# A graph network kernel: first edge tiles gathered at each group's first edge for the dense build

## The reference, cut to what matters

```python
dst = jnp.minimum((6250 * jax.random.uniform(key3, (200000,)) ** 2.0).astype(jnp.int32), 49999)
_o = jnp.argsort(dst, stable=True); src = src[_o]; dst = dst[_o]
...
x = _layernorm(x + _L0(x, src, dst, ...))     # three propagations: sum over edges of (x * norm)[src] into dst
x = _layernorm(x + _L1(x, edge_attr_64, ...)) # an MLP per edge, summed into dst
x = _layernorm(x + _L2(x, src, dst, w, ...))  # twice: segment_sum(w[:, None] * h[src], dst), then hyperbolic normalisation
x = _layernorm(x + _L3(x, src, dst, ...))     # one propagation with degree norms
```

## Time and profile before

| | us |
|---|---|
| median of 3 runs | 6,764.94 |
| lowest, highest | 6,760.87, 6,765.24 |
| the profiled execution | 6,769.59 |
| its span, first to last instruction | 6,767.8 |
| mean granted TensorE clock, share of full | 0.837 |

### The profile page before, as it was taken

One profiled execution on the slowest core, in us unless ns is written; L12 is line 12 of the kernel. 1 busy time (PEld: TensorE's weight loads), 2 busy tenths in 40 slices (PEclk: granted clock), 3 DMA queues, 4 the chain that ended last, 5 costly groups with the idle time before them and its releaser, 6 DMA issues.

```text
span 6767.8 us, 158522 instructions
## 1 busy us (share of the span) xinstructions
PE 4832.8 (71%) x47510; PEld 3804.9 (56%) x47511; DVE 3362.4 (50%) x6082; ACT 1317.2 (19%) x3392; POOL 2135.5 (32%) x3522
## 2 busy tenths in 40 slices
PE   0999988877777777998936666666666667657475
PEld 0777776666666667998924444444444433323275
DVE  7989888777777774012134444444444420020323
ACT  0122233445555552000011111111111100000100
POOL 1222222222222221000027777777777720000000
PEclk9999999999999998999965556555555579989887
DMA  1011123333343343988753333333333359969575
GB/s 36 19 52 56 57 68 100 105 116 123 123 140 122 125 137 127 388 345 337 283 108 79 79 78 78 78 78 79 79 79 79 79 190 418 379 276 418 233 289 194
DMA packets 443092, 1053.75 MB, mean 156 GB/s; under 512 B 129847, under 2 KB 286849, under 8 KB 414081
## 3 DMA queue, kind: packets, MB, share of 16 engines
q1 hardware_dynamic: 392770, 1000.83, 41.3%
q0 software_dynamic: 50176, 51.48, 4.1%
HBM read 809.69 MB, written 242.41 MB: 155 GB/s over the span
## 4 chain that ended last, share of the span: by engine, by line
PE 33%; POOL 19%; DVE 14%; issue 12%; DMA 11%; POOLq 7%; ACT 2%; SPq 1%; ACTq 1%; DVEq 0%; PEldq 0%; PEld 0%
POOL WORK L624 18%; PE banks L1525 13%; PE banks L1486 12%; DMA T<-dense_w 8%; POOLq L350 4%; PE banks L1517 3%; DVE T L828 3%; DVE T L835 2%; PE banks L1556 2%; DMA WORK<-table,idx 2%; POOLq L581 1%; ACTq L346 1%; POOLq L590 1%; POOL T L581 1%; DVE WORK L922 0%
## 5 line engine op out<-in xcount | busy, mean ns | idle before, releaser
L624 POOL DMA_INDIRECT WORK<-table,idx x1568 | 1486.6, 948 | 1357.1 <-DVE idx L928 879.6
L1525 PE MATMUL banks<-T 128*128 128x125 bf16 (+1 forms) x21696 | 1672.9, 226 | 48.0 <-DVE T L835 8.8
L1525 PEld LDWEIGHTS banks<-T 128*128 128x128 bf16 x21696 | 1447.2, 115 | 341.5 <-DVE T L835 326.1
L828 DVE TENSOR_TENSOR T<-T 128x750 bf16<-128x750 bf16 x1808 | 995.3, 550 | 457.8 <-PE banks L1525 319.2
L581 POOL TENSOR_TENSOR T<-T 128x12 f32 x1816 | 567.4, 312 | 1818.6 <-DVE T L835 1250.6
L835 DVE TENSOR_TENSOR T<-T 128x750 bf16<-128x750 bf16 x1808 | 1002.0, 554 | 62.0
L1517 PE MATMUL banks<-T 128*128 128x250 bf16 x3616 | 711.8, 278 | 411.6 <-DVE T L828 142.9
L1486 PE MATMUL banks<-WORK,T 125*128 125x192 bf16 (+1 forms) x10000 | 835.0, 247 | 61.2 <-DVE WORK L972 61.2
L1486 PEld LDWEIGHTS banks<-WORK,T 125*128 125x128 bf16 (+1 forms) x10000 | 832.4, 99 | 63.7 <-issue 59.2
L1443 PE MATMUL banks<-T,WORK 128*128 x1568 | 275.4, 294 | 768.3 <-DVE WORK L884 768.3
L1283 ACT ACTIVATE WORK<-banks 125x252 f32<-125x252 f32 x1250 | 477.4, 382 | 1541.3 <-PE banks L1525 1470.0
(11 more groups left out here) (339 smaller groups left out, 3474.4 us busy)
## 6 DMA issues: line engine op xcount, KB each, us to landing
T<-dense_c SPq DMA_DIRECT2D x200, 1562.5 KB, 8.3
T<-dense_w SPq DMA_DIRECT2D x200, 782.0 KB, 10.3
T<-dense_w SPq DMA_DIRECT2D x200, 780.5 KB, 10.4
dense_w<-WORK SPq DMA_DIRECT2D x250, 546.9 KB
WORK<-rel_rows SPq DMA_DIRECT2D x197, 256.0 KB, 3.7
WORK<-in_eaT SPq DMA_DIRECT2D x392, 128.0 KB, 3.5
dense_c<-T SPq DMA_DIRECT2D x13, 3125.0 KB, 10.5
dense_c<-ACC SPq DMA_DIRECT2D x12, 3125.0 KB, 10.7
```

The lines of the kernel that those rows point to most:

```text
L624: nc.gpsimd.indirect_dma_start(out=g_sb[:, u, c * D:(c + 1) * D], out_offset=None, in_=table, in_offset=bass.IndirectOffsetOnAxis(ap=idx[: ...
L828: V.tensor_tensor(planes[:, v, 0:HOTS].rearrange("p (k n t) -> p k n t", k=3, t=QUAD), iota2[:, 0:LO, :].unsqueeze(1).to_broadcast([P, 3, ...
L1525: last = T.matmul(banks[:, u, to - low // QUAD:to + LO + high // QUAD], keys[:, t, j, :], planes[:, v, first - low:past + high].rearrange( ...
```

## The change

Each group gets one tile that is gathered from HBM, its first tile. Groups of 128 edges or fewer get the 128 edges from the group's first edge on, so one tile holds them all. Larger groups get their first whole column, and their further columns as before come from SBUF. For this the range stage turns keys, lows and weights to rows (three numbers an edge, `RECORD`), ScalarE copies them, and SP stores them in HBM (`edges_dram`). Each set now has 125 rows of ten groups, by `q` = group modulo ten. For each set GpSimd fetches the columns in which groups begin and end (`ends`), VectorE finds the first and last edge in them (`ends_of`), and ten indirect DMAs gather the first tiles (`got_rows`); TensorE turns them back, ScalarE and VectorE put them in `firsts`, with keys relative to the group and the weight in three parts.

The dense build then runs in units of four groups (`UNIT`): VectorE makes the planes of four first tiles with one call each for one-hots and products; TensorE puts each in a PSUM bank of its own (eight banks, two units). Groups go in blocks of two. A block has as many further steps as its larger group needs; a step (`more`) takes one column of each of the two groups, prepared by two GpSimd subtractions. A group that needs fewer is pointed at empty columns. The loops over steps are dynamic on GpSimd, VectorE and TensorE, which read a table of offsets. ScalarE copies two banks at once and a store holds ten groups, in place of five. `xT` is loaded after the dense build, and `sel` filled there.

```diff
+sp.wait_ge(edges_copied, TURNED)
+sp.dma_start(edges_dram[0:full * P, :].rearrange("(t p) x -> p t x", p=P), edge_rows[:, 0:full, :, :].rearrange("p t e k -> p t (e k)")).then_inc(edges_stored, 16)
...
+sp.dma_start(X[:], xT).then_inc(x_loaded, 16)
...
+pool.wait_ge(edges_stored, 32)
+for q in range(SETS):
+    if q >= 2:
+        pool.wait_ge(range_step, at_range(0, f"members{q - 2}"))
+    pool.wait_ge(range_step, at_range(0, f"hi_int{q}"))
+    for h, col in enumerate((lo_int, hi_int)):
+        nc.gpsimd.indirect_dma_start(
+            out=ends[:, q % 2, h, :, :].rearrange("p e k -> p (e k)"), out_offset=None, in_=edges_dram,
+            in_offset=bass.IndirectOffsetOnAxis(ap=col[:, q:q + 1], axis=0)).then_inc(ends_landed[q % 2], 16)
+pool.wait_ge(range_step, at_range(0, "start_int"))
+for q in range(SETS):
+    nc.gpsimd.indirect_dma_start(
+        out=got_rows[:, q, :, :].rearrange("p e k -> p (e k)"), out_offset=None, in_=edges_dram.rearrange("c (e k) -> (c e) k", k=RECORD),
+        in_offset=bass.IndirectOffsetOnAxis(ap=start_int[:, q:q + 1], axis=0)).then_inc(firsts_landed[q], 16)
 nc.gpsimd.memset(ACC_full[3 * P // 4:P, :], 0.0).then_inc(tails_cleared, 1)
+nc.gpsimd.memset(T1_full[3 * P // 4:P, TURNED * (P // 2):NP], 0.0).then_inc(tails_cleared, 1)
...
+def take(s, b, deltas):
+    slot = pool.snap(s & (QRING - 1), min_val=0, max_val=QRING - 1)
+    at = []
+    for t in range(QUAD):
+        pool.reg_alu(col[t], s + deltas[QUAD * b + t], COLS, ALU.min)
+        at.append(nc.s_assert_within(pool.snap(col[t]), 0, COLS, skip_runtime_bounds_check_because="a column is never before the first"))
+    pool.wait_ge(more_products, s + 1)
     pool.sem_inc(quads_begun, 1)
-    nc.gpsimd.tensor_tensor(quads[:, ds(slot, 1), :, :].rearrange("p s k t -> p (s k) t"), lists[:, :, ds(col, QUAD)],
-                            starts[:, u, :].unsqueeze(2).to_broadcast([P, 6, QUAD]), ALU.subtract).then_inc(quad_taken, 1)
-
-with pool.Fori(0, GROUPS // SPAN) as i:
-    bounds = bounds_of(pool, i * SPAN, SPAN)
...
+    for b in range(BATCH):
+        with pool.If(offs[b + 1] > offs[b]):
+            with pool.Fori(offs[b], offs[b + 1]) as s:
+                take(s, b, row[BATCH + 1:])
+    pool.wait_ge(quad_taken, offs[BATCH] + 1)
...
+        fin(V.tensor_scalar(g_back[:, col], g_lo[:, col], 1.0, -1.0, ALU.max, ALU.mult))
+        at(f"back{q}")
+        fin(V.tensor_scalar(g_lo[:, col], g_back[:, col], float(COLS), None, ALU.add))
+        fin(V.tensor_scalar(lo_int[:, col], g_back[:, col], float(COLS), None, ALU.add))
+        at(f"from{q}")
+        fin(V.scalar_tensor_tensor(g_hi[:, col], g_lo[:, col], 1.0, g_hi[:, col], ALU.add, ALU.max))
+        at(f"up{q}")
+        fin(V.tensor_scalar(hi_int[:, col], g_hi[:, col], -1.0, None, ALU.add))
+
+    def ends_of(q):
+        col = slice(q, q + 1)
+        keys = ends[:, q % 2, :, :, 0]
+        dve.wait_ge(ends_landed[q % 2], 32 * (q // 2 + 1))
+        fin(V.tensor_scalar(met.rearrange("p (h e) -> p h e", h=2), keys, g_first[:, col], None, ALU.is_ge))
+        at(f"past{q}")
+        fin(V.scalar_tensor_tensor(met_too.rearrange("p (h e) -> p h e", h=2), keys, g_last[:, col], met.rearrange("p (h e) -> p h e", h=2), ALU.is_le, ALU.mult))
+        at(f"members{q}")
+        fin(V.tensor_tensor_reduce(met_last, back_no, met_too[:, 0:P], 1.0, 0.0, ALU.mult, ALU.max, g_n[:, col]))
+        at(f"first{q}")
+        fin(V.tensor_tensor_reduce(met_last, one_no, met_too[:, P:2 * P], 1.0, 0.0, ALU.mult, ALU.max, g_off[:, col]))
+
+    for q in range(SETS + 1):
...
+    fin(V.tensor_scalar(g_small, g_less, float(2 * P), None, ALU.is_le))
...
+    fin(V.scalar_tensor_tensor(g_hi, g_hi, -1.0, g_less, ALU.add, ALU.mult))
...
+    fin(V.tensor_reduce(block_more, g_hi.rearrange("p (b t) -> p b t", t=QUAD), AX, ALU.max))
+    fin(V.scalar_tensor_tensor(g_lo, g_small, float(FAR), g_lo, ALU.mult, ALU.add))
...
+        step = lambda n: dve.wait_ge(firsts_step, q * 3 + n)
+        dve.wait_ge(firsts_copied, q + 1)
+        for j in range(2):
+            V.scalar_tensor_tensor(to[:, j, :], keys, -float(KEYS * q + LO * j), group_row, ALU.add, ALU.subtract)
+        if q:
+            step(0)
+        V.tensor_tensor(w_rest, w, to[:, 3, :], ALU.subtract).then_inc(firsts_step, 1)
+        step(1)
+        V.tensor_copy(to[:, 4, :], w_rest).then_inc(firsts_step, 1)
+        step(2)
+        V.tensor_tensor(to[:, 5, :], w_rest, to[:, 4, :], ALU.subtract).then_inc(firsts_step, 1)
...
+    def more(s, x):
+        quad = quads[:, ds(s & (QRING - 1), 1), :, :].rearrange("p s k t -> p (s k) t")
+        dve.wait_ge(quad_taken, s + 2)
+        dve.wait_ge(more_used, s + 1)
+        one_hots(more_planes[:, x, :], QUAD, iota2, quad[:, 0:3, :]).then_inc(more_hots, 1)
+        dve.wait_ge(more_hots, s + 1)
+        products(more_planes[:, x, :], QUAD, quad[:, 3:6, :]).then_inc(more_products, 1)
...
+    def unit(u, v, offs):
+        dve.wait_ge(first_used, u * 2 + 2)
+        one_hots(first_planes[:, v, :], UNIT, iota4, firsts[:, 0:3, ds(u * UNIT, UNIT)]).then_inc(first_hots, 1)
+        dve.wait_ge(first_hots, u + 1)
+        products(first_planes[:, v, :], UNIT, firsts[:, 3:6, ds(u * UNIT, UNIT)]).then_inc(first_products, 1)
+        dve.wait_ge(more_used, offs[0] + SLOTS)
+        dve.sem_inc(mores_begun, 1)
+        for h, (begin, past) in enumerate(zip(offs, offs[1:])):
+            with dve.If(past > begin):
+                with dve.Fori(begin, past, 2) as s:
+                    more(s, 2 * h)
+                    with dve.If(past > s + 1):
+                        more(s + 1, 2 * h + 1)
+
+    with dve.Fori(0, UNITS // 2) as i:
...
+        act.wait_ge(firsts_step, (q - 1) * 3)
+    got = banks[:, 4 + q % 4, 0:RECORD * P].rearrange("p (k n) -> p k n", k=RECORD)[:, :, 0:LO]
+    C.activation(raw[:, q % 2, :, :], got[:, 0::2, :], ACT.Copy)
...
+        act.wait_ge(first_used, n * BATCH + (b + 1 + 2 * SLOTS))
+        act.wait_ge(more_used, past[b] + SLOTS)
+        both = banks[0:LO, 2 * ((j * BATCH + b) % TURN):2 * ((j * BATCH + b) % TURN) + 2, :]
+        C.activation(dense_out[0:LO, b0, 2 * b:2 * b + 2, :], both[:, :, KEYS:KEYS + 2 * WCOLS], ACT.Copy)
+        C.activation(counts_out[slot][0:LO, :, d:d + QUAD * GROUP].rearrange("p h (g d) -> p g d h", g=QUAD), both[:, :, 0:KEYS].rearrange("p g (d h) -> p g d h", h=HI), ACT.Copy).then_inc(block_copied, 1)
...
+    def more(s, x, bank):
+        plane = more_planes[:, x, :]
+        pe.wait_ge(more_hots, s + 1)
         for t in range(QUAD):
-            T.matmul(banks[:, u, 0:KEYS], lows[:, t, :], hot[:, t, 0:KEYS], start=begins and t == 0, stop=False, skip_group_check=True)
-        pe.wait_ge(pair_ready, now)
+            counts_of(plane, QUAD, t, bank + t, False)
+        pe.wait_ge(more_products, s + (1 + QRING))
...
+    def unit(u, v, offs):
+        plane, blocks = first_planes[:, v, :], len(offs) - 1
+        pe.wait_ge(first_hots, u + 1)
+        for h in range(blocks):
+            pe.wait_ge(block_copied, u * 2 + (h + 1))
+            for t in range(QUAD * h, QUAD * h + QUAD):
+                counts_of(plane, UNIT, t, UNIT * v + t, True)
+        pe.wait_ge(first_products, u + 1)
+        for h in range(blocks):
+            for t in range(QUAD * h, QUAD * h + QUAD):
+                last = weights_of(plane, UNIT, t, UNIT * v + t)
+            last.then_inc(first_used, 1)
```

More of the change, by code:

```diff
@@ L587, in _ @@
+            with pool.Fori(0, ROWS) as i:
+                row = loads(pool, rows_sb[0:1, ds(i * TABLE, TABLE)], -BLOCKS * COLS, BLOCKS * COLS)
+                offs = [nc.s_assert_within(pool.snap(v & MASK), 0, BLOCKS * COLS, skip_runtime_bounds_check_because="they were worked out within them") for v in row[0:BATCH + 1]]
                 pool.wait_ge(starts_set, i + 1)
                 pool.sem_inc(spans_begun, 1)
[L589 to L591 removed]
```

446 lines of the change are left out of this document (245 added, 201 removed).

## The result

| | us |
|---|---|
| before, median on this chip | 6,763.56 |
| after, median of 4 runs (lowest, highest) | 6,870.67 (6,868.18, 6,882.47) |
| ratio, 95% interval | 1.0162, 1.0145 to 1.018 |
| span of the profiled execution after | 6,870.9 |

The forecast was 6,100 us, with a range of 5,900 to 6,450.

What follows compares the result with a forecast made beforehand. VectorE, with TensorE close, bounds the early build and GpSimd's sequencer the late one. Build 2,452 to 11 + 1,300 + 30 + 403 = 1,744 us (-708), +33 before, +3 behind: 6,769.6 becomes 6,098, rounded 6,100; range 5,900 to 6,450.

Steps and rivals of the forecast that it cites:

- counts copy: ScalarE's copy of the counts in the dense build, two banks by one call: 0.459 us goes to 0.67, 0.59 if free.
- first tile on TensorE: Matmuls in the dense build: 0.48 us a tile at full clock, 1,167 us for all 2,432 tiles.
- load of five values on ScalarE: Register load in the dense build, priced at 0.58 us from PE, within ScalarE's 7.1 us per ten groups.
- VectorE's unit: Four groups' first tiles in the dense build: two calls of 0.92 us plus register load, branches and waits, 2.4 us.
- late stretch: The 280 blocks without further steps: 7.2 us per ten groups, bounds 5.9 and 8.5, 403 us in all.
- GpSimd's step: Preparing a further step of two tiles: 1.5 us, bounds 0.83 and 2.0; GpSimd paces the first 345 blocks at 1,300 us.
- VectorE's step: VectorE's calls and loop for a further step in the first 345 blocks: 1.35 us, between 1.1 and 1.6.
- Rival (b): Gaps hold TensorE's clock at half level in the build: +339 us, 6,440; 18%, shared with GpSimd steps of 1.8 to 2.3.
- wrong at the root: Named failure: steps not 591, or stride-four first tiles over 0.48 us on TensorE; 0.1 us more is 125 us where uncovered.
- rival (a): VectorE paces the first half if a GpSimd step costs 1.2 us or less: 6,010, or down to 5,840; 20%.
- Rival (c): Slower than before, by GpSimd's step in the dense build costing over 2.6 us; slower 3%.
- Before the build: Range stage and gathers up to the barrier: +33 us, bounds 15 and 55; barrier at 185 us.

Runs made afterwards that it cites:

- runs of ten: Changed kernel with the counts copy's loops reordered to write ten neighbouring two-byte numbers instead of single ones 500 bytes apart; 6,460.4 us, ratio 0.9542.
- planes in pairs: Kernel with runs of ten, a unit's four first tiles held as two planes of two interleaved tiles; 6,784.18 us on a slower chip, ratio 0.9299.
- three removals: From planes in pairs with one load a block (first part 1,432 us): a VectorE call, eight matmuls or a GpSimd subtraction dropped per step; at most 8 us shorter.

## Why the prediction was wrong, by its steps

| step | forecast | measured |
|---|---|---|
| steps, matmuls, VectorE calls | 591; 14,592; 313 and 591 | the same |
| VectorE calls of 1,500 | 0.92 us | 0.942 |
| counts copy | 0.67 us | 2.39 |
| first tile on TensorE | 0.48 us | 0.94 |
| load of five values on ScalarE | 0.58 us | 2.3 (median) |
| VectorE's unit | 2.4 us | 4.8; 3.6 after the repairs |
| late stretch, ten groups | 7.2 us | 16.2; 10.4 and 8.8 after the repairs (runs of ten, planes in pairs) |
| first 345 blocks | 1,341 us | 1,594; 1,512 and 1,390 after the repairs |
| GpSimd's step | 1.5 us | 0.98 |
| VectorE's step | 1.35 us | 1.30 |
| barrier ahead of the build | 185 us | 191.4 |

**The counting was right.** Tiles, steps, matmuls and calls came out to the unit. What failed were prices: of two instructions whose layout the change made new, of a register load, and of VectorE's unit and GpSimd's step.

**The counts copy.** The step "the counts copy, 0.459 for 250, goes to 0.67 (its output is now strided the other way; 0.59 if free)" is the one that turned the sign. I had seen the new order and given it 0.08 us; it cost 1.8. Its bounds were no bounds: 0.59 to 0.67 came from copies that write side by side or in runs of five, and no row that I read writes two-byte numbers singly. It was worth 327 us late and 82 us early. With it TensorE waited, and its clock was granted at 0.60 late, where with runs of ten it was 0.88. Rival (b) came true as a consequence, not as a cause: with planes in pairs and the copy as it was, TensorE was busy 105 us less and the clock stood at 0.67, and ScalarE still set 16 us per ten groups (899 us). The Trainium skill (TensorE: Matmul & The Clock Gate, section HAM oscillation) warns of gaps that cost clock; here, other than in before, the trace agrees, by the 0.60 beside 350 us of waits.

**The stride of four.** The last part named this as the way to be "wrong at the root", at 0.1 us a tile; it was 0.46. Before read every plane with a stride of two, so the earlier trace rows priced a different read. The sum carried it at 0.48 without a bound above, and no rival held it. It was worth 85 to 88 us late and 122 early once the copy was mended; with the copy as it was, 90 us early and 11 late, since ScalarE covered the rest. The Trainium skill (SBUF — State Buffer, section Door 1: The DMA port swizzle) says that memory is read by lines of 16 bytes and that bandwidth is full as long as two accesses fall in a line. Four bf16 numbers are 8 bytes, two reads in a line, so by that rule the stride would be free; these runs show 0.94 us a tile at four and, by the medians above, 0.53 with only the moving operand at two. The measurement decides.

**The load.** The earlier trace rows gave 0.58 us for PE, and I used it for ScalarE. The same rows had 2.3 us as the median on GpSimd. The lower price was taken without a reason. 56 loads of 2.55 us (143 us in the late stretch with both repairs) in place of 0.58 are 110 us, an estimate, more than the 91 to 94 that this stretch lacks; no run had cheaper loads. Stores did not pace it: the DMA share was 0.68, and ScalarE waited for them for 18 us.

**Who paces the first half.** I took GpSimd, at 1.5 us a step, against VectorE at 1.35. Where GpSimd ran free in after, before its ring was full, its pairs of subtractions started 0.98 us apart, the time of its register work:

```profile
208.40 0.62 POOL L654 TENSOR_TENSOR T<-T 128x6 f32 x2 [0.29 <-issue]
209.38 0.66 POOL L654 TENSOR_TENSOR T<-T 128x6 f32 x2 [0.36 <-issue]
210.37 0.53 POOL L654 TENSOR_TENSOR T<-T 128x6 f32 x2 [0.32 <-issue]
```

So rival (a) named the engine rightly, and its condition (1.2 us or less) was met; its time was wrong by the same prices. VectorE's step was right, its unit was not: (1,390 - 591 x 1.30) / 172.5 = 3.6 us a unit, forecast 2.4. Of it 2.2 are calls; the rest is the register load every second unit, what a fresh unit waits for after it, and waits for TensorE, and was not split further. In after the same sum gives 4.8, with 250 us of waits for TensorE's slow first tiles among it.

**Before the build.** 39 us in place of 33, inside the bounds of 15 and 55. Two small calls lasted long beside GpSimd's fills, as forecast from the earlier trace rows:

```profile
167.38 5.60 POOL L623 MEMSET ACC<- 32x6400 f32 x1
...
169.62 3.66 DVE L917 CAST NORM<-WORK 128x125 bf16<-128x125 f32 x1
```

The six us over come with the ten sets of firsts, which ran on to the barrier after the fills were done at 178 us (2.45 us a set). VectorE held them: from 178.3 to 190.4 us it was busy for 11.8 of 12.1 us, and ScalarE waited 0.89 us for it in each set. So a copy with the same fault as the counts copy was hidden here: ScalarE writes 250 two-byte numbers 20 bytes apart in 1.28 us, and its neighbour's 250 four-byte numbers side by side in 0.41.

```profile
L1403 ACT ACTIVATE NORM<-banks 128x250 bf16<-128x250 f32 x10 | 12.8, 1282 | 0.0
...
L1402 ACT ACTIVATE WORK<-banks 128x250 f32<-128x250 f32 x10 | 4.1, 411 | 127.6 <-PE banks L1738 114.2 <-DVE NORM L919 13.4
```

**Behind the build.** 4,176 us where before had 4,165: +11, forecast +3.

**The chances.** 3% for slower was far too little. Rival (c), the one case on that side, was about GpSimd. Three prices were taken from rows of another layout or another engine and given next to no room, and each came out dearer: 410 and 208 us measured by repairs and 110 by the estimate above, together more than the whole forecast gain of 672.

## What to carry to other kernels

When a change lays data out anew, price every instruction that reads or writes the new layout from a row with the same element width and the same stride; if there is none, the price is open upward and belongs into the range and among the rivals. Let the innermost loop of a two-byte write run over neighbours, even if the read side (PSUM here) becomes strided instead, and keep TensorE's moving operand at a stride of two bf16 numbers rather than four, even at the price of more VectorE calls. The repaired kernel shows that the idea was sound: with these two edits it takes 0.930 of the time of before, 517 and 519 us less, on the two slower chips where it was timed.

To find what paces a stretch, adding work tells more than taking it away: three removals changed nothing, one of them because the removed call had covered register work and a second engine stood close behind.

## What the runs showed of the hardware that I had not expected

- ScalarE, PSUM to SBUF, 125 partitions: 500 two-byte numbers take 0.59 us in runs of ten and 2.39 us singly, 500 bytes apart; 250 take 0.46 in runs of five and 1.285 singly (1.28 also 20 bytes apart, 128 partitions); 250 four-byte numbers singly take 0.65. The first of these reads PSUM with a stride, and takes as long as 504 four-byte numbers read and written side by side beside it (0.594 and 0.596).
- TensorE: six matmuls of 125 columns and one of 250 take 0.48 us a tile with the moving operand at a stride of two bf16 numbers and 0.94 at four; the stationary operand at four and eight in place of two and four costs little (late stretch 582 against 575 us). At four the matmuls of 125 columns start 119 ns apart (median) in both late stretches, the one granted 0.88 of the clock and the one granted 0.60.
- A load of 5 registers on ScalarE takes 0.54 us at least and 2.3 in the median, one of 25 takes 15.6.
- With its matmuls thinned out TensorE was granted 0.75 of its clock in place of 0.92, in a stretch that something else paced, and so looked nearly as busy (998 of 1,431 us for 8,394 matmuls) as with all of them (1,100 of 1,432 for 13,122): a busy share without the clock beside it says little.
